# The experts' weight loads of a mixture-of-experts kernel, issued by GpSimd instead of the sync engine

## The reference, cut to what matters

```python
def L1(x, t_emb, router_W, router_bias, w1, w3, w2, W1e, W2e):     # D, HS, HE, E, K = 512, 1024, 512, 8, 2
    shared = silu(xf @ w1) * (xf @ w3) @ w2
    s = sigmoid(concat([xf, tf]) @ router_W)
    _, topk_idx = top_k(s + router_bias, 2)
    gates = s_sel / s_sel.sum()
    h = gelu(einsum('nc,ech->enh', xf, W1e))
    y = einsum('enh,ehc->enc', h, W2e)
    routed = einsum('ne,enc->nc', combine, y)
    return (shared + routed) / 3
x = x + L0(x, cond, ...)     # a layer with a weight per batch entry
x = x + L1(x, cond, ...)
```

## Time and profile before

| | |
|---|---|
| median of three runs | 1178.25 us (1171.87 to 1181.19) |
| the profiled execution: time | 1181.49 us |
| its span | 1179.5 us |
| TensorE busy | 1096.6 us, 93% of the span |
| VectorE, ScalarE, GpSimd busy | 482.2, 393.8, 164.3 us |
| DMA | 191.41 MB, 162 GB/s over the span |
| start of the matmuls of group 0 | 315.72 us |
| start of the matmuls of the last group (15) | 687.70 us |

### The profile page before, as it was taken

One profiled execution on the slowest core, in us unless ns is written; L12 is line 12 of the kernel. 1 busy time (PEld: TensorE's weight loads), 2 busy tenths in 40 slices (PEclk: granted clock), 3 DMA queues, 4 the chain that ended last, 5 costly groups with the idle time before them and its releaser, 6 DMA issues.

```text
span 1179.5 us, 15385 instructions
## 1 busy us (share of the span) xinstructions
PE 1096.6 (93%) x5226; PEld 878.3 (74%) x5226; DVE 482.2 (41%) x1015; ACT 393.8 (33%) x687; POOL 164.3 (14%) x200
## 2 busy tenths in 40 slices
PE   6999899999469999999989999999999999999998
PEld 5666677778357777777767777888888888888886
DVE  4103644543335446554655445133333314233334
ACT  2212444521335555655555543121212111121211
POOL 3002175640200000000000002202020110202020
PEclk8999999999779999999999999999999999999999
DMA  8562599868966775667556733405040120404040
GB/s 309 230 250 97 183 334 351 303 232 238 324 192 177 200 187 142 178 195 191 148 166 197 181 133 108 178 1 178 1 166 12 63 114 0 178 0 178 0 143 36
DMA packets 119157, 191.41 MB, mean 162 GB/s; under 512 B 9534, under 2 KB 58686, under 8 KB 117334
## 3 DMA queue, kind: packets, MB, share of 16 engines
q1 hardware_dynamic: 105670, 149.03, 40.9%
q0 software_dynamic: 13456, 41.95, 9.6%
HBM read 117.04 MB, written 73.92 MB: 162 GB/s over the span
## 4 chain that ended last, share of the span: by engine, by line
PE 55%; DMA 15%; DVE 12%; SPq 7%; issue 7%; ACT 2%; POOL 1%; ACTq 0%; DVEq 0%; POOLq 0%
DMA xr<-xs_d 12%; PE K L1445 5%; PE K L1447 5%; PE K L1446 5%; PE M L1445 4%; PE M L1446 4%; PE M L1447 4%; SPq L419 3%; DVE xt L1298 3%; PE Rb L1535 3%; PE L L1447 2%; PE L L1446 2%; PE L L1445 2%; PE Rb L1447 2%; PE Rb L1446 2%
## 5 line engine op out<-in xcount | busy, mean ns | idle before, releaser
L1445 PE MATMUL M<-w2h,gTh 128*128 128x512 f32 x256 | 102.2, 399 | 17.5 <-DVE gTl L475 17.5
L460 ACT ACTIVATE slf<-K 128x512 f32<-128x512 f32 x64 | 38.3, 599 | 226.7 <-PE K L1447 222.3
L756 POOL DMA_INDIRECT yb<-ys_d,pos_fix x64 | 61.0, 953 | 327.6 <-DVE total L1376 309.6
L1446 PE MATMUL M<-w2l,gTh 128*128 128x512 f32 x256 | 101.7, 397 | 0.0
L1447 PE MATMUL M<-w2h,gTl 128*128 128x512 f32 x256 | 101.7, 397 | 0.0
L463 ACT CAST gTh<-slf 128x512 fp32r<-128x512 f32 x64 | 39.7, 621 | 184.0 <-DVE slf L473 184.0
L1447 PE MATMUL K<-x1h,w13l 128*128 128x512 f32 x256 | 101.0, 395 | 0.0
L1445 PE MATMUL K<-x1h,w13h 128*128 128x512 f32 x256 | 100.3, 392 | 0.7 <-DVE x1l L1425 0.7
L1446 PE MATMUL K<-x1l,w13h 128*128 128x512 f32 x256 | 100.2, 391 | 0.0
L1298 DVE STREAM_TRANSPOSE xt<-xr 128x512 f32<-128x512 f32 x64 | 45.0, 705 | 111.2 <-DMA xr<-xs_d 111.0
L473 DVE TENSOR_TENSOR slf<-L,slf 128x512 f32<-128x512 f32 x32 | 22.1, 691 | 163.9 <-PE L L1447 155.3
(11 more groups left out here) (246 smaller groups left out, 2492.0 us busy)
## 6 DMA issues: line engine op xcount, KB each, us to landing
w2c<-in_L_cond_w_dram SPq DMA_DIRECT2D x8, 2048.0 KB, 8.4
e1raw<-in_L_cond_W1e_dram SPq DMA_DIRECT2D x16, 1024.0 KB, 5.7
xr<-xs_d SPq DMA_DIRECT2D x64, 256.0 KB, 7.3
e2raw<-in_L_cond_W2e_dram SPq DMA_DIRECT2D x16, 1024.0 KB, 8.2
ys_d<-yo SPq DMA_DIRECT2D x32, 512.0 KB, 2.9
xtok<-in_x_dram SPq DMA_DIRECT2D x32, 256.0 KB, 7.4
x_d<-x1tok SPq DMA_DIRECT2D x8, 1024.0 KB, 8.1
xs_d<-zeros SPq DMA_DIRECT2D x8, 1024.0 KB, 8.1
```

The source lines that it names most:

```text
L756: pool.indirect_dma_start(out=yb[:, c, :], out_offset=None, in_=ys_d, in_offset=bass.IndirectOffsetOnAxis(ap=pos_fix[:, c:c + 1].bitcast(U ...
L1445: mm(o, ah, bh_, start=start, stop=False)
L1446: mm(o, ah, bl_, start=False, stop=False)
```

## The change

The two loading functions go from SP's program to GpSimd's, in a loop over the groups of its own. The first e1 and e2 are issued as soon as the table is there and the scatters are done, ahead of the zero blocks of `ys_d`, which no longer wait for the first e1. In the loop GpSimd waits for the cut of e1 and loads the next, waits for the cut of e2 and loads the next. SP keeps the pads, the rows, the stores of y and all that follows.

```diff
@@ SP
-            load_e1(0)
             sp.wait_ge(pad_out, 16 * E)
             load_rows(0)
-            load_e2(0)
 
             def load_group(g, n):
                 if n is not None:
-                    sp.wait_ge(e1_lo, n * KC)
-                    load_e1(n)
                     sp.wait_ge(xt_f, n * TT)
                     load_rows(n)
-                    sp.wait_ge(e2_lo, n * KC)
-                    load_e2(n)
@@ GpSimd
-            pool.wait_ge(e1_in, 16)
+            pool.wait_ge(tab_in, 16)
+            for b in range(NB):
+                tok_left(pool, b)
+            for i in range(EARLY):
+                pool.wait_ge(x1T_out[i], 16 * ((NB - 2 - i) // EARLY + 1))
+            pool.wait_ge(wsl, PIECES)
+
+            def load_e1(g):
+                row = value(pool, EROW, g, (E - 1) * KC)
+                pool.dma_start(e1raw[:], w1e_view[:, ds(row, KC), :]).then_inc(e1_in, 16)
+
+            def load_e2(g):
+                row = value(pool, EROW, g, (E - 1) * KC)
+                pool.dma_start(e2raw[:], w2e_view[:, ds(row, KC), :]).then_inc(e2_in, 16)
+            load_e1(0)
+            load_e2(0)
 
             for g in range(SURE, GROUPS_MAX):
                 pool.dma_start(ys_d[g * GR:(g + 1) * GR, :]..., zero_src).then_inc(ys_zero, 16)
 
-            pool.wait_ge(tab_in, 16)
-            last = value(pool, LAST, 0, GROUPS_MAX - 1, 1)
+            def load_weights(g, n):
+                if n is not None:
+                    pool.wait_ge(e1_lo, n * KC)
+                    load_e1(n)
+                    pool.wait_ge(e2_lo, n * KC)
+                    load_e2(n)
+            last = groups(pool, load_weights)
             pool.wait_ge(tabs, 3)
```

More of the change, by code:

```diff
@@ L593, in _ @@
             sp.sem_inc(y_out[1], YO_FREE)
[L595 to L601, removed]
             def load_rows(g):
```

## The result

| | before | after |
|---|---|---|
| median of 13 runs | 1177.71 us | 1186.41 us |
| ratio of the runs | | 1.0073 (1.0054 to 1.0093) |
| profiled execution: time, span | 1181.49, 1179.5 us | 1185.25, 1183.7 us |
| start of group 0, group 1, group 15 on TensorE | 315.72, 352.84, 687.70 us | 350.89, 374.87, 691.83 us |

The change made the kernel 0.7% slower; 1163.6 was forecast. The spans divide as follows. Up to the start of group 1 the kernel lost 374.87 - 352.84 = 22.0 us. From group 1 to group 15 it gained 334.86 - 316.96 = 17.9 us. Behind group 15 nothing changed (491.9 against 491.8 us). 22.0 - 17.9 + 0.1 = 4.2.

What follows compares the result with a forecast made beforehand. The experts' late rows, through VectorE and ScalarE, were taken to hold TensorE back. A gain of 26.9 us in the groups less 12.2 lost ahead of them made -14.7, so a median of 1163.6 us, range 1153 to 1176.

Steps and rivals of the forecast that it cites:

- What bounds the kernel: Experts' stage: late rows delay VectorE, then ScalarE's copy of y; groups take 23.92 us against TensorE's own 22.0.
- Part 1: Groups' loop: with weight loads off SP, rows come 4.1 us earlier and TensorE bounds 14 groups, gaining 26.9 us.
- e1 is free to go when e1 of g is cut, which VectorE has done before the group starts: In the groups: the next e1 flows at about 473 to 477 us, beside the stores of y, as hidden work.
- Part 2: Ahead of group 1: first loads and zero blocks come earlier and delay the pads' end; 12.2 us lost.
- the zeros: Ahead of the pads' end: 7.34 MB, 18.9 to 22.0 us by earlier rates, taken as 20.5.
- the three loads: Ahead of the pads' end: three weight loads of 1.05 MB at 380 GB/s, 8.3 us.
- The cold start: Group 0 on TensorE: after an idle stretch the clock is 0.50, which costs 2.5 us.
- Two queues together had shares of 107.5%: Pads beside zeros and loads: overlap of two queues over some 33 us gives back 2.3 us.
- The mixture is slow: Rival ahead of group 1: pads and zeros move at only 216 GB/s, pads end at 357, 1193 us; chance 0.07.
- issue time only: Rival in the groups: e1 still flows when rows start, gain 18.5 instead of 26.9 us, 1172 us; chance 0.12.
- slower: Outcome for the whole kernel: a median over 1190.0 us; chance 0.08.
- e1 on GpSimd's queue taking longer than 5 us: Sign in the groups: e1 taking this long from issue to use would show the prediction wrong.

Runs made afterwards that it cites:

- x3: Changed kernel, but GpSimd waits for the last pad before its first e1 and e2, and for e1's landing before the zeros: 1178.65 us, 1.0003 of the kernel before.
- x1: Changed kernel with GpSimd's seven zero blocks issued at 17 us, long before the table, instead of beside the pads: 1157.65 us, 0.9807 of the kernel before.
- x4: Changed kernel with GpSimd's zeros held until the last pad has landed, first e1 and e2 still beside the pads: 1173.98 us, 0.9953 of the kernel before.
- y4: x1 with the rows also issued by GpSimd, between e1 and e2, and group 0's e2 behind the last pad: 1153.99 us, 0.9614 of the kernel before.
- z4: y4 run once more, on a third chip where the kernel before takes 1204.44 us: 1162.34 us, ratio 0.9643.

## Why the prediction was wrong

- **What bounds the kernel: right.** The groups are held back by `xr` through VectorE and ScalarE, and TensorE's pace is the floor. The floor is 21.76 and not 22.0, and a whole group on it would have brought 14 x (23.92 - 21.76) = 30.2 us.
- **Part 1, the 26.9 us of the groups: this step failed in its second half.** The rows were to be there 4.1 us earlier, with 2.7 us to spare. In the first groups they were: VectorE waited 2.33 us instead of 6.33 to 7.57, and the rows were used 10.55 us into the group instead of 14.70, the 4.1 us of the sum. The step "e1 is free to go when e1 of g is cut, which VectorE has done before the group starts" took that moment for fixed. It is not: in this kernel the last cut of e1 stands behind the third transpose, so it moves with the rows. The spare time shrinks by 0.5 to 1.3 us a group and then is gone. From group 6 on the rows are used 14.0 to 14.3 us into the group, 0.4 to 0.7 us earlier than before, where the sum itself had asked for 1.4. The wait that was left out is that of the stores of y behind a late e1: I had e1 "beside the stores of y" at no cost. 17.9 us came instead of 26.9, and in x3, whose groups start badly, 11.7.
- **Part 2, the 12.2 us lost: right mechanism, wrong size.** 22.0 were lost. The last pad landed at 336.7 and not at 327.3. The mis-sized term is the zeros: 20.5 us in the sum, 27.7 measured by x1, with x1's faster pads in it. I had priced 7.34 MB at 334 to 388 GB/s, what that queue did beside loads of e1 and of rows. Beside pads the two queues together moved 278 GB/s. At 278 the zeros are 26.4 us and the three loads 11.3. The cold start was 23.98 - 21.76 = 2.2 us, 2.5 in the sum.
- **"Two queues together had shares of 107.5%", 2.3 us given back: wrong.** Here the shares sum to 94%.
- **The rivals.** "The mixture is slow", at 0.07, came in part, at 278 and not at 216 GB/s: the pads were done 9.4 us later than in my sum, short of the 342 from which it alone would decide. The rest came from "issue time only", in part and for a reason that I had not named. I had asked of each whether it alone turns the sign, and not what both do together: 9.8 + 9.0 = 18.8 us against a margin of 14.7. And 0.07 with half of 0.04 + 0.03 is 0.105, not the 0.08 that I gave to "slower".
- **The rest of the miss.** The medians miss by 1186.4 - 1163.6 = 22.8 us, the profiled executions by 1185.2 - 1166.8 = 18.4. The other 4.4 are the executions: I let the one after lie 3.2 us above its median, and it lies 1.2 below.
- **A sign badly chosen.** "e1 on GpSimd's queue taking longer than 5 us" told nothing: from issue to landing it is 5.8 us in the fast groups already, and 5.7 on SP before.
- **The rule of the Trainium skill** ("DMA: Bandwidth & Descriptors", "Issuing engines are not separate DMA queues": several issuing engines save only the issue time) is nearer to what was seen than my sum: 18.5 us by the rule and 17.9 measured. That is chance: the same loop brought 11.7 us in x3 and 22.0 in x4 (366.14 to 679.01), and its first four groups gained 2.2 us each, more than the 1.3 of the issue. And y4 and z4, which differ from the changed kernel's loop only in who issues the rows and when, show all of it, 21.76: a wait that stands before an issue on one engine and not on the other is worth more than the issue.

## What to carry to other kernels

Before a load is moved to another queue, ask when its buffer is freed and whether that moment moves with the very thing that the load competes with: a gain that shrinks a little in each round ends at another fixed point. Read several rounds and not one. Look next at the order of the consumers: putting work that was ready ahead of work that waits for a late transfer gave 2.7% with no DMA moved, where moving the loads of the weights gave nothing on the same chip. And bytes that nobody waits for (here 7.3 MB of zeros) belong where the DMA has time, not where their issuer happens to be free.

## What the runs showed of the hardware

- Pads of 0.5 KB packets alone moved 271 GB/s over their whole stretch, and 283 inside it (272 to 290 us). Together with GpSimd's zeros of about 4 KB (10.49 MB in 2720 packets, with the weights) both moved 278. The two streams of writes did not add up. Zeros beside loads had shown 337 and 318 GB/s in all. But the pads' own rate is not one number: x4 shows 347 GB/s from 285 to 291 us and 284 from 298 to 306, both times pads alone. What decides it is open.
- The queue with the large packets wins. Beside the zeros, 1 MB of rows in small packets needed 27 us from issue to use (x4: 13.3% of the engines for SP's queue). "DMA: Bandwidth & Descriptors" of the Trainium skill, section "Queues, rings and completion order", says that each engine takes turns between queues by packets. The trace agrees where both queues have work all the time: 1991 packets against 1990 in the changed kernel from 281 to 311 us. In x4 it is 1742 against 2047, in a stretch at whose start zeros were still few (135 against 640 from 313 to 316 us). It does not agree beside a single load of e1: there the stores of y on SP's queue, issued at 484.78, had got no packet by 488.54, while in group 1 theirs came within 1.3 us of the issue at 374.54. By what unit the turns go was not tried.
- The same kernel took 1178 us on one chip and 1202 to 1204 on two others. It lies in the first stage: the changed kernel's first pad goes out at 290.00 on the third chip and at 270.35 on the first, and group 0 starts at 370.98 and 350.89. The ratio of the change differed too: 1.0073 and 0.9997. What makes the difference was not tried.
